# Query projections of a banded attention: all columns of four heads ahead of the first unit, or half the columns, and the rest in pairs of heads

## The reference, cut to what matters

```python
t = t + _L2_attn_ref(_ln_t(t), Wq, Wk, Wv, Wu, bu)

def _L2_attn_ref(x, Wq, Wk, Wv, Wu, bu):       # x: 16 images, 256 tokens, 32 channels
    xp = jnp.pad(x, ((0, 0), (k - 1, 0), (0, 0)))
    q = (x @ Wq.T).reshape(b, t, h, e) / scale
    kk = (xp @ Wk.T).reshape(b, tp, h, e) / scale
    v = (xp @ Wv.T).reshape(b, tp, h, e)
    idx = jnp.arange(t)[:, None] + jnp.arange(k)[None, :]
    dot = jnp.einsum('bthe,btkhe->bthk', q, kk[:, idx])
    attn = jax.nn.softmax(dot, axis=-1)
    out = jnp.einsum('bthk,btkhe->bthe', attn, v[:, idx])
    return out.reshape(b, t, h * e) @ Wu.T + bu
```

## Time and profile before

| what | us |
|---|---|
| median of 3 runs | 662.25 (661.84 to 662.41) |
| the profiled execution | 661.13 |
| its span, first to last instruction | 659.5 |
| VectorE busy | 482.1 |
| TensorE busy (matmuls) | 432.4 |
| GpSimd busy | 355.6 |
| ScalarE busy | 201.9 |

### The profile page before, as it was taken

The page is one execution under the profiler, slowest core; times in us unless marked ns, Lnnn a source line. Parts: engine busy times, 40 slices in busy tenths (PEclk is TensorE's granted clock), DMA queues, the critical chain, the costliest instruction groups (busy, mean ns, idle before and its releaser), DMA issues.

```text
span 659.5 us, 8992 instructions
## 1 busy us (share of the span) xinstructions
PE 432.4 (66%) x3396; PEld 225.7 (34%) x3406; DVE 482.1 (73%) x615; ACT 201.9 (31%) x222; POOL 355.6 (54%) x290
## 2 busy tenths in 40 slices
PE   6655774218767676776776888788277998645660
PEld 2442223203222222222222335566244664532220
DVE  2956995698999999999999325999515534996332
ACT  2562594023333323323322244312020007212110
POOL 6536406969999999999999000477860000240000
PEclk8857796658999999999999989655566998558856
DMA  8350011524555555555552000000010000000000
GB/s 290 40 231 0 10 52 29 128 79 146 159 146 144 157 143 147 158 144 145 159 144 49 1 11 1 1 2 2 1 21 1 0 1 1 1 3 4 7 5 32
DMA packets 29256, 46.10 MB, mean 70 GB/s; under 512 B 17878, under 2 KB 19320, under 8 KB 28184
## 3 DMA queue, kind: packets, MB, share of 16 engines
q1 hardware_dynamic: 26776, 45.10, 24.1%
q0 software_dynamic: 2368, 0.37, 0.5%
q10 hardware_dynamic: 64, 0.00, 0.0%
HBM read 43.55 MB, written 1.11 MB: 68 GB/s over the span
## 4 chain that ended last, share of the span: by engine, by line
POOL 31%; DVE 22%; PE 19%; issue 16%; SPq 4%; ACT 4%; DMA 2%; DVEq 0%; POOLq 0%; ACTq 0%
POOL dBu L878 14%; POOL hit L865 9%; PE ps L1913 3%; SPq L657 3%; PE ps L2220 2%; POOL work L927 2%; PE ps L2123 2%; POOL work L925 2%; POOL work L914 2%; PE ps L2231 2%; POOL hst L627 1%; DVE work L1681 1%; PE ps L2392 1%; PE ps L2382 1%; DMA work<-in_L_attn_edge_index 1%
## 5 line engine op out<-in xcount | busy, mean ns | idle before, releaser
L1109 ACT ACTIVATE ps<-work,a_neg 128x1020 f32<-128x1020 f32 x64 | 71.3, 1115 | 164.7 <-DVE hst L1450 99.1
L2051 PE MATMUL ps<-hC,ident 128*128 128x512 f32 x256 | 120.9, 594 | 0.0
L1450 DVE TENSOR_TENSOR_SCAN hst<-ps,dBu 128x1024 f32<-128x1024 f32 x43 | 98.2, 2285 | 4.1 <-ACT ps L1109 1.3
L2035 PE MATMUL ps<-late,pick_state 96*128 96x512 bf16 x128 | 39.5, 391 | 85.8 <-DVE hC L1468 67.7
L878 POOL TENSOR_TENSOR dBu<-work,dA 128x1024 f32<-128x1024 f32 x32 | 75.6, 2363 | 2.8 <-DVE hst L1450 2.2
L878 POOL TENSOR_TENSOR dBu<-work,b_sb 128x1024 f32<-128x1024 f32 x32 | 75.9, 2374 | 0.6
L865 POOL DMA_INDIRECT hit<-in_L_attn_edge_values,tab_i x64 | 63.5, 992 | 12.8 <-issue 10.0
L2051 PEld LDWEIGHTS ps<-hC,ident 128*128 128x128 f32 x256 | 48.9, 191 | 42.6 <-issue 33.5
L2035 PEld LDWEIGHTS ps<-late,pick_state 96*128 96x128 bf16 x128 | 7.7, 97 | 136.9 <-DVE hC L1468 116.7
L959 POOL TENSOR_TENSOR work<-work 128x1024 f32<-128x1024 f32 x3 | 5.7, 1912 | 85.7 <-DVE work L1690 85.7
L1468 DVE TENSOR_TENSOR hC<-hst,ps 128x1024 f32<-128x1024 f32 x43 | 51.4, 1194 | 0.8 <-PE ps L2035 0.8
(11 more groups left out here) (361 smaller groups left out, 868.8 us busy)
## 6 DMA issues: line engine op xcount, KB each, us to landing
b_sb<-b_rows_all SPq DMA_DIRECT2D x64, 256.0 KB
dA<-b_rows_all SPq DMA_DIRECT2D x64, 256.0 KB
work<-in_L_attn_edge_index SPq DMA_DIRECT2D x6, 1024.0 KB, 6.5
dA<-in_L_attn_edge_index SPq DMA_DIRECT2D x1, 1024.0 KB, 10.3
dBu<-in_L_attn_edge_index SPq DMA_DIRECT2D x1, 1024.0 KB, 12.3
hit<-in_L_attn_edge_values,tab_i POOLq DMA_INDIRECT x64
late<-work SPq DMA_DIRECT2D x12, 64.0 KB, 2.0
X<-in_x SPq DMA_DIRECT2D x1, 512.0 KB, 3.8
```

What stands on the lines that cost most here:

```text
L1109: nc.scalar.activation(dst[:, :, 1:], src[:, :, 1:], ACT.Exp, scale=a_neg[:, n:n + 1]).then_inc(dA_sb, 1)
L1450: V.tensor_tensor_scan(h_buf[i % 3], dA_ps[k], dBu[:, k, :], 0.0, ALU.mult, ALU.add).then_inc(scan_done, 1)
L2035: last = T.matmul(bank(2 + h), pick_state[:, n, :, :].rearrange("p v i -> p (v i)"), parts[:, j * NT + h * HALF:j * NT + (h + 1) * HALF], ...
L2051: last = T.matmul(bank(6 + h), ident[:, :], hC[:, i % 2, h * HALF:(h + 1) * HALF], start=False, stop=(n == S - 1))
```

## The change

A projection of a head now covers one half of the columns (two sets) and one bank. Ahead of unit 0 only the first halves of heads 0 to 3 are projected, into banks 4 to 7, as soon as the first half of `xpad` is written; TensorE waits for the second half after that. The other twelve half projections are done as six pairs, each two heads of one half in banks 6 and 7, copied by one instruction of 1024 columns. The pairs take the places of heads 4 to 7 in units 0 and 1 and the same places in unit 2. The scores of units 0 and 1 wait for the first four copies, those of each later two units for two pairs more. The clearing of the output banks moves from unit 2 to unit 3.

```diff
-        QM_BANK = (0, 2, 4, 6) + (6,) * 4
+        QM_PAIRS = ((0, 1), (2, 1), (4, 0), (6, 0), (4, 1), (6, 1))
+        QM_READY = 4 + len(QM_PAIRS)
...
-            def query_heads(h):
+            def first_queries(h):
                 act.wait_ge(qm_ps, h + 1)
-                nc.scalar.activation(qm[:, :, h, :], bank(QM_BANK[h], 2).rearrange("p (t q) -> p t q", q=C),
+                nc.scalar.activation(qm[:, 0:2 * WT, h, :], bank(4 + h).rearrange("p (t q) -> p t q", q=C),
+                                     ACT.Copy).then_inc(qm_sb, 1)
+
+            def query_pair(k):
+                h, i = QM_PAIRS[k]
+                act.wait_ge(qm_ps, 4 + k + 1)
+                nc.scalar.activation(qm[:, 2 * WT * i:2 * WT * (i + 1), h:h + 2, :].rearrange("p t h q -> p h t q"),
+                                     bank(6, 2).rearrange("p (h t q) -> p h t q", h=2, q=C),
                                      ACT.Copy).then_inc(qm_sb, 1)
...
             for h in range(4):
-                query_heads(h)
+                first_queries(h)
             window_keys(0)
             for u in range(UNITS):
-                if u < 2:
-                    query_heads(4 + 2 * u)
+                if u < 3:
+                    query_pair(2 * u)
...
-                if u < 2:
-                    query_heads(5 + 2 * u)
+                if u < 3:
+                    query_pair(2 * u + 1)
...
             stream_norm(3, 2, 4)
+            pe.wait_ge(normed, 2 * 2 - 1)
+            pe.wait_ge(w2_sb, 1)
+
+            def project(k, h, i):
+                return T.matmul(bank(k), w_km[:, h, :], xpad[:, 2 * i:2 * i + 2, C:], start=True, stop=True)
+
+            def project_pair(k):
+                h, i = QM_PAIRS[k]
+                pe.wait_ge(qm_sb, 4 + k)
+                project(6, h, i)
+                project(7, h + 1, i).then_inc(qm_ps, 1)
+
+            for h in range(4):
+                project(4 + h, h, 0).then_inc(qm_ps, 1)
             pe.wait_ge(normed, 2 * 2)
-            pe.wait_ge(w2_sb, 1)
-
-            def project(h):
-                k = QM_BANK[h]
-                for i in range(2):
-                    last = T.matmul(bank(k + i), w_km[:, h, :], xpad[:, 2 * i:2 * i + 2, C:],
-                                    start=True, stop=True)
-                last.then_inc(qm_ps, 1)
-
-            for h in range(4):
-                project(h)
...
             def clear_outputs():
-                pe.wait_ge(qm_sb, H2)
+                pe.wait_ge(qm_sb, QM_READY)
...
             def unit_scores(u):
                 hg, j = unit(u)
-                if u == 0:
-                    pe.wait_ge(qm_sb, 4)
-                else:
+                pe.wait_ge(qm_sb, 4 + u // 2 * 2)
+                if u > 0:
                     pe.wait_ge(s2_read, u)
...
             for u in range(UNITS):
-                if u < 2:
-                    pe.wait_ge(qm_sb, 4 + 2 * u)
-                    project(4 + 2 * u)
+                if u < 3:
+                    project_pair(2 * u)
                 unit_values(u, 1)
                 if u < UNITS - 1:
                     unit_scores(u + 1)
-                if u < 2:
-                    pe.wait_ge(qm_sb, 5 + 2 * u)
-                    project(5 + 2 * u)
-                if u == 2:
+                if u < 3:
+                    project_pair(2 * u + 1)
+                if u == 3:
                     clear_outputs()
```

## The result

657.62 us median (655.7 to 659.8, 12 runs) against 662.37 (659.5 to 666.65, 12 runs of the kernel before on the same chip): ratio 0.9934, interval 0.9916 to 0.9953, so 4.4 us faster (3.1 to 5.6). The forecast was 657.2.

What follows compares the result with a forecast made beforehand. One file of work ahead of the loop was taken to bound the kernel: 661.13 - 5.03 (1.16 + 3.44 + 0.43, other terms 0) = 656.10, plus 1.12 to the median, gave 657.2 us, range 655.4 to 660.0.

Steps and rivals of the forecast that it cites:

- What bounds the kernel: Ahead of the loop: a single file of work, so bringing unit 0's scores forward brings the whole loop forward.
- The part ahead of unit 0: Before unit 0's scores: earlier start, four projections instead of eight, shorter last copy; 5.03 us earlier in all.
- 1.16 + 3.44 + 0.43: Ahead of unit 0: 1.16 us from the earlier start, 3.44 from fewer projections, 0.43 from the shorter last copy.
- an estimate of 0.72: ScalarE's 512-column copy ahead of unit 0, priced by the skill at 0.72 us; the prediction took 0.60.
- Units 0 and 1 as a rigid shift: Units 0 and 1: pairs replace heads 4 to 7 with the same work and order, so no time is added.
- The pair copy's pattern: 1024-column copies in units 0 and 1: extra pattern dimension taken as free; at most 0.37 us a copy, 1.1 in all.
- Unit 2's two pairs at 0: Unit 2: two added pairs cost 0, covered by the key copy's wait for VectorE, with 1.0 us of cover left.
- the prediction's own sign of being wrong: Units 0 to 2: a granted clock of 0.50 anywhere between 388 and 416 would show the forecast wrong.
- The rival that was given 4 to 10 in 100: Units 0 to 2: TensorE's clock falls earlier; slower 0.04, nothing or a lost unit 2 together 0.06.
- the row that spoke against it: A stretch without a projection, 402.46 to 405.56, kept the clock at 1.00, against an earlier clock fall.
- 5.6 or 6.4: Cost of an earlier clock fall: 5.6 us in unit 2, some 6.4 for a whole unit 0 or 1.
- Behind the loop: After the loop's last sum: the gain passes through; clock changes taken as 0, about 1.3 us earlier or 2.3 later possible.

Runs made afterwards that it cites:

- halves_ahead: Changed kernel with all eight half projections of heads 0 to 3 ahead of unit 0 and no pairs in unit 2; 661.01 us, ratio 0.9977.
- both_first: Changed kernel, but TensorE waits for both halves of the normalised input before its first projection; 657.45 us, ratio 0.9933 to the kernel before.
- cover9: Changed kernel with nine filler matmuls of 512 columns ahead of pair 4 in unit 2; 654.00 us in a single execution.
- third_look: Changed kernel unaltered, run for a third trace; 657.12 us in a single execution.
- again: Changed kernel unaltered, run for a second trace and more times; 656.75 us, ratio 0.9904 to the kernel before.
- mixed: Changed kernel with one set of heads 0 to 3 ahead of unit 0, their second in its first slot, then the six pairs; 656.64 us, ratio 0.9929.
- moved32: Changed kernel with 32 one-column matmuls on TensorE ahead of the last three outputs; 660.66 us, ratio 0.9986 to the kernel before.
- the quarters: Changed kernel with one 256-column set of heads 0 to 3 ahead of unit 0, seven sets in later slots; 658.63 us, unaltered rerun 659.34 us.

## Why the prediction was right

- *What bounds the kernel.* One file of work ahead of the loop, so that time taken off it goes through: halves_ahead and both_first moved the scores by 3.33 and 1.17 and the sum behind the loop by 3.33 and 1.19.
- *The part ahead of unit 0*: forecast 1.16 + 3.44 + 0.43 = 5.03, measured 4.94 at the scores and 4.91 over the loop. The start was worth 1.17 (both_first). From the first projection to the last copy's start the chain has 3.74 (389.42 to 393.16) instead of 7.17, so 3.43 less (forecast 3.44), and a half copy took 0.597 against the 0.60 taken. The 0.09 that is missing lies behind that copy: the scores began 0.13 after its end (393.77 to 393.90) instead of the 0.05 of the forecast, which no run explains; it is also what makes halves_ahead, with 0.05 there, 3.33 later and not 3.43. The Trainium skill's price for ScalarE (ScalarE: Activation LUTs, Rules for kernel authors), which gave the prediction an estimate of 0.72, is stated for a bias that is a pointer operand, and this copy has none: the measured 0.597 decides.
- *Units 0 and 1 as a rigid shift*: 6.35 and 6.57 between merges in a trace without a fall, 6.36 and 6.56 before. The pair copy's pattern is free, 1.023.
- *Unit 2's two pairs at 0*: 8.41 against 8.40, the key copy released by VectorE, and 1.1 us of cover by cover9 (1.0 forecast).
- *The clock.* Here the prediction's own sign of being wrong, a clock of 0.50 between 388 and 416, came in the first trace. The rival that was given 4 to 10 in 100 is the step that was mis-sized, and both ways. A fall happens in about half of the traces of the changed order, not rarely; the row that spoke against it (1.00 from 402.46 to 405.56) was one execution: the same stretch, 398.30 to 401.40 in the changed kernel's first trace, was followed by a fall, and the kernel before has one of its own, a slot earlier, in its second trace. And it costs 1.67 us (0.8 in the kernel before), not 5.6 or 6.4, because the clock was back after one slot (3.60 against 1.93) and the rest of the unit ran at 1.00. "The default state is throttled, and activity releases the throttle", in the Trainium skill's words (TensorE: Matmul & The Clock Gate, What's actually happening), agrees with falls behind values and scores (to 0.50 at about 401.6) and a return behind a projection (to 1.00 at about 405.0). Which execution has one, no run settles: third_look has the same order of work and none. Half of 1.67 for the changed kernel and a third of 0.8 for the order of before (1 of 3 traces, halves_ahead among them) take some 0.6 off 4.91, an estimate of 4.3; the times gave 4.4 (3.1 to 5.6) and, in again, 6.4 (3.9 to 8.9), which hold 4.9 as well. So that the forecast of 657.2 met 657.62 so nearly is in part luck: the sum is right to 0.1 in a trace without a fall, and the falls that it left out are small.
- *Behind the loop* 0 was taken with 1.3 down and 2.3 up; the five traces of the unaltered kernels lie from 174.4 to 176.4 there. That, the start of the normalisation (387.9 to 389.9) and the falls go far to explain why single executions of one kernel lie 4 to 7 us apart.

## What to carry to other kernels

Where a loop's first unit needs only part of what is prepared ahead of it, move the rest into slots that wait for another engine, and price the slots by the cover that is left until another engine's wait ends (here 1.1 us on TensorE). Let no unit need what the slot just ahead of it makes: in mixed that cost 0.8. Measure such a change from a fixed event ahead of it to one behind it in traces with the same granted clock in that stretch; times of whole executions needed a dozen runs for 4 us, the trace gave it to 0.1. And before dropping a variant whose part got faster while the whole did not, look far behind the change, where nothing was edited.

## What the runs showed that was not expected

Thirty-two one-column matmuls, 1.01 us of work in a wait, cost some 3 us of time: 128 us later a string of matmuls pauses at a place that goes by the number of TensorE's instructions before it (1.2 to 1.9 us behind the 118th in three traces with 32 more records, 0.47 behind the 115th with 35, none in the others). Loading of code fits: the page's instruction queue has 30 packets, of 16 KB each, in these kernels and 29 in the unaltered ones. But cover9 and mixed have 30 too and no pause there, so the number of loads isn't it; where one falls may be. The traces have the packets' times. In all four traces with a pause the packet that the unaltered kernels lack starts 1.12 to 1.15 us behind the pause's end (at 595.49 in moved32, where the pause ends at 594.37), and none starts within the pause; in mixed and cover9 it starts 3.4 and 4.4 us behind the end of the string. So the pause isn't a wait for that packet, but the two belong together, as if TensorE stepped from one block of code to the next there. The Trainium skill calls the cost of crossing a 16 KiB boundary of code "mostly hidden" and warns that a taken branch breaks the prefetch (Runtime: NRT & Kernel Launch, Instruction fetch mechanics); the layers whose steps are chosen by the data begin some 7 us behind this string. That the pause comes from the loading of code was argued, not shown.

In moved32 the rest is a lower clock just behind the pause. Four matmuls of 512 columns behind the string, first in moved32, then in the first trace of the changed kernel:

```profile
596.33 3.37 PE L1922 MATMUL ps<-X,centerer 128*128 128x512 f32 x4
...
594.25 2.13 PE L1922 MATMUL ps<-X,centerer 128*128 128x512 f32 x4
```

From the half sum beside the string to the choice of the next step (VectorE, L1739 to L1754) moved32 took 12.1 us and that trace 8.6: 1.87 of the 3.5 between them is the pause, and the clock, at 1.00 until the pause was over, was 0.53 from 596.33 to 599.50. The two traces of the quarters took 12.5 and 12.7, at 0.50 already through the string (118 matmuls in 1.82 us instead of 1.21). But third_look, without a pause, was at 0.50 there too and took 11.1, so that the pause brings the fall isn't shown.

A stall can also give something back: in cover9 the 0.82 us lost at unit 3's merge came back by 0.55 in the next unit. Timelines of VectorE (first row) and GpSimd (second row) in unit 3, first the changed kernel:

```profile
423.13 2.06 DVE L1557 TENSOR_TENSOR work<-work,mx 128x1024 f32<-128x1024 f32 x1
...
422.03 2.08 POOL L928 TENSOR_TENSOR work<-work,band 128x896 f32<-128x896 f32 x1
```

then cover9:

```profile
421.62 1.22 DVE L1557 TENSOR_TENSOR work<-work,mx 128x1024 f32<-128x1024 f32 x1
...
419.41 2.09 POOL L928 TENSOR_TENSOR work<-work,band 128x896 f32<-128x896 f32 x1
```

VectorE's subtraction takes 2.06 us where GpSimd's band multiplication runs beside it (422.03 to 424.11) and 1.22 where that is already over (419.41 to 421.50). The delay moved the subtraction past it. The 0.98 that GpSimd still had to run (424.11 - 423.13) and 1.22 would be 2.20, near the 2.06; the Trainium skill (SBUF — State Buffer, SBUF: two separate sides) has an operation of VectorE with both inputs in SBUF wait for one of GpSimd that reads there and began first, which the rows agree with. No run took GpSimd's work away, so that it is the neighbour that slows it rests on these pairs of rows.
